# The scan of a two-layer sequence kernel: z, v and u moved by pairs of octets

## The chip, the cores and the metric

The kernel runs on one core of one Trainium2 chip. The metric is the device time of one execution in microseconds, as a median over runs. Before the change it is 2332.63 us, median of 3 runs that lie between 2332.56 and 2332.96.

The core has TensorE (PE, with its weight loads shown apart as PEld), VectorE (DVE), ScalarE (ACT), GpSimd (POOL) and SyncE (SP). SP does no arithmetic here; it issues nearly all DMA transfers, in program order.

## The reference

Two layers over x (2 batches, 4096 positions, 512 channels, f32). The change lies in the first layer, in its recurrence:

```python
Abar = sigmoid(A)                      # A: 512 channels x 16 states
def step(h, xt):                       # h: batch x channels x states
    h = h * Abar + xt[..., None] * B_ssm
    y = einsum('bcs,cs->bc', h, C_ssm) + D_ssm * xt
    return (h, y)
x1 = x @ w1_w.T + w1_b
x_ssm = _ssm(silu(_depthwise_conv(x1, conv_w)), A, B_ssm, C_ssm, D_ssm)
v = silu(x @ v1_w.T + v1_b)
return x_ssm * v @ w2_w.T + w2_b
```

Beside it the first layer has a product with weights and inputs quantised to a 6-bit grid in blocks of 32; the second has a linear attention with 16 heads and a gated feed-forward net. Both layers start with a layer norm and add onto x.

## The kernel before, in words

The program has four phases one after the other, with a barrier of all engines between them: project (`x @ w1`, `x @ v1`, convolution, silu; results go to DRAM as `scr_z` and `scr_v`), scan (the recurrence), mix (the rest of layer 1 and the start of layer 2) and second_layer. The change is in scan, `phase_scan` at L509, which takes from 418.04 to 608.76 us of the profiled span.

The scan works on octets: 8 channels at a time, so 64 octets (`NO`). The 4096 positions of a batch are cut into chunks of 16. For one octet, z is a tile of 128 partitions (8 channels x 16 places in a chunk) by 512 columns (2 batches x 256 chunks), 256 KB in f32. The work on octet o is:

- POOL spreads three tables of the octet into 128x128 matrices: `into`, `toep`, `outof` (L580, three tables in turn, `TABS`).
- PE `own(o)` (L673): z times `into`, into one of two banks `SB`. It gives each chunk's own contribution to the state at its end.
- DVE `scan(o)` (L590): two scans along the chunks give the `state`.
- PE `Y(o)`, as this text calls it: z times `toep` (L690) and then `state` times `outof` (L693), both into one of two banks `YB`.
- DVE `gate(o)` (L596): `YB` times v, written over v. This is u.

A product of f32 appears in the trace as two matmul records. PE runs in the order own(o+1), Y(o); DVE in the order scan(o+1), gate(o). In the first nine octets DVE also does one step of the quantisation of a weight after each gate (L610 to L632; five of the nine take about 2.3 us); ACT loads four weight matrices of 1 MB at the start of the phase (L654 to L658), and PE turns one of them in octets 24 to 27 (L680).

SP loads z (`zo`, 4 buffers) and v (`vo`, 5 buffers), one transfer of 256 KB per octet each, and stores u from the v buffer. `load(o)` waits, for a z buffer, until the Y that read it is complete (`y_full`), and for a v buffer until the store of u from it has landed (`u_stored`). Octets 0 to 3 are loaded at once; after that, each turn of SP's loop waits for gate(o) (`u_done`), stores u of o, and loads octet o+4 (`load(o + 3)` at the head of the next turn). The phase ends when all stores have landed (L568).

Of the kernel before, what the change touches and what calls it, by code (L numbers as in the profile page):

```python
# [3 lines left out]
P = 128  # L4
# [3 lines left out]
ALU = mybir.AluOpType  # L8
# [16 lines left out]
OCTET = 8  # L25
# [483 lines left out]
def phase_scan(nc, sh, ins, scr, keep, banks, mem, late):  # L509
    KT, D, NO, NCB, NCH, NS, B = sh.KT, sh.D, sh.NO, sh.NCB, sh.NCH, sh.NS, sh.B  # L510
    sb = mem.tile
    Z, V, TABS = 4, 5, 3

    def sem(name):
        return nc.alloc_semaphore(name)

    zo = [sb(f"c_z{i}", [P, NCH]) for i in range(Z)]
    vo = [sb(f"c_v{i}", [P, NCH]) for i in range(V)]
    state = [sb(f"c_state{i}", [P, B, NCB]) for i in range(2)]
    into = [sb(f"c_into{i}", [P, OCTET, NS]) for i in range(TABS)]  # L520
    toep = [sb(f"c_toep{i}", [P, OCTET, CHUNK]) for i in range(TABS)]
# [9 lines left out]
    z_in = [sem(f"c_z_in{i}") for i in range(Z)]  # L531
    v_in = [sem(f"c_v_in{i}") for i in range(V)]
    u_stored = [sem(f"c_u_stored{i}") for i in range(V)]
# [3 lines left out]
    y_full, u_done = sem("c_y_full"), sem("c_u_done")  # L537
# [5 lines left out]
    SB, YB, FB = banks[0:2], banks[2:4], banks[4:8]  # L543
    into_t, toep_t, out_pow, mask8 = keep["into_t"], keep["toep_t"], keep["out_pow"], keep["mask8"]
    ident = keep["ident"]
    z_of = scr["z"].rearrange("(o c) r n -> o (c r) n", c=OCTET)
    v_of = scr["v"].rearrange("(o c) m n -> o (c m) n", c=OCTET)
    u_of = scr["u"].rearrange("(o c) m n -> o (c m) n", c=OCTET)
    TURN_AT = 24

    def sync(sp):
        def load(o):
            if o >= Z:
                sp.wait_ge(y_full, o - Z + 1)
            sp.dma_start(zo[o % Z][:, :], z_of[o]).then_inc(z_in[o % Z], 16)
            if o >= V:
                sp.wait_ge(u_stored[o % V], 16 * (o // V))
            sp.dma_start(vo[o % V][:, :], v_of[o]).then_inc(v_in[o % V], 16)

        for o in range(3):  # L560
            load(o)
        for o in range(NO):
            if o + 3 < NO:
                load(o + 3)
            sp.wait_ge(u_done, o + 1)
            sp.dma_start(u_of[o], vo[o % V][:, :]).then_inc(u_stored[o % V], 16)
        for i in range(V):
            sp.wait_ge(u_stored[i], 16 * len(range(i, NO, V)))  # L568

    def gpsimd(pool):  # L570
        nc.gpsimd.memset(keep["kv"][:, :, :, :], 0.0).then_inc(keep["set"], 1)
# [11 lines left out]
    def vector(dve):  # L583
        def scan(o):
            dve.wait_ge(own_full, o + 1)
            if o >= 2:
                dve.wait_ge(y_full, o - 1)
            rate = keep["decay"][:, o:o + 1].broadcast_to([P, NCB - 1])
            for b in range(B):
                nc.vector.tensor_tensor_scan(state[o % 2][:, b, 1:], rate, SB[o % 2][:, b * NCB:(b + 1) * NCB - 1],  # L590
                                             0.0, ALU.mult, ALU.add).then_inc(state_done, 1)

        def gate(o):
            dve.wait_ge(y_full, o + 1)
            dve.wait_ge(v_in[o % V], 16 * (o // V + 1))
            nc.vector.tensor_tensor(vo[o % V][:, :], YB[o % 2][:, :], vo[o % V][:, :], ALU.mult).then_inc(u_done, 1)  # L596

        def weight_low(i, kt, tile, raw):
            dve.wait_ge(w_hi, KT * i + kt + 1)
            nc.vector.tensor_tensor(tile[:, 1, kt, :], raw[:, kt, :], tile[:, 0, kt, :].bitcast(F32),  # L600
                                    ALU.subtract).then_inc(w_lo, 1)

        blocks = wf_nat[:, :].rearrange("p (b e) -> p b e", e=QBLOCK)
        NB = KT * D // QBLOCK

        def wide(tile):
            return tile[:, :].unsqueeze(2).broadcast_to([P, NB, QBLOCK])

        def quantise_step(k):
            dve.wait_ge(wf_in, 16)  # L610
            if k:
                dve.wait_ge(q_step, k)
            if k == 0:
                ins_ = nc.vector.tensor_reduce(q_max[:, :], blocks, AX.X, ALU.max, apply_absolute_value=True)
            elif k == 1:
                ins_ = nc.vector.tensor_scalar(q_scale[:, :], q_max[:, :], 1.0 / FP6_MAX, SCALE_EPS, ALU.mult, ALU.max)
            elif k == 2:
                ins_ = nc.vector.reciprocal(q_inv[:, :], q_scale[:, :])
            elif k == 3:
                ins_ = nc.vector.tensor_tensor(blocks, blocks, wide(q_inv), ALU.mult)  # L620
            elif k == 4:
                ins_ = nc.vector.tensor_scalar(q_work[:, :].bitcast(U32), wf_nat[:, :].bitcast(U32), EXPONENT_BITS,
                                               None, ALU.bitwise_and)
            elif k == 5:
                ins_ = nc.vector.tensor_scalar(q_work[:, :], q_work[:, :], 1.0, ROUND_MAGIC, ALU.max, ALU.mult)
            elif k == 6:
                ins_ = nc.vector.tensor_tensor(wf_nat[:, :], wf_nat[:, :], q_work[:, :], ALU.add)
            elif k == 7:
                ins_ = nc.vector.tensor_tensor(wf_nat[:, :], wf_nat[:, :], q_work[:, :], ALU.subtract)
            else:  # L630
                ins_ = nc.vector.tensor_tensor(blocks, blocks, wide(q_scale), ALU.mult)
            ins_.then_inc(q_step, 1)  # L632

        for i in range(2):
            nc.vector.memset(state[i][:, :, 0:1], 0.0).then_inc(zeroed, 1)
        dve.wait_ge(zeroed, 2)
        scan(0)
        for o in range(NO):
            if o + 1 < NO:
                scan(o + 1)  # L640
            gate(o)
            if o < 9:
                quantise_step(o)
            if TURN_AT <= o - 2 < TURN_AT + KT:
                kt = o - 2 - TURN_AT
                dve.wait_ge(f_hi, kt + 1)
                nc.vector.tensor_tensor(wf[:, 1, kt, :], FB[kt][:, :], wf[:, 0, kt, :].bitcast(F32), ALU.subtract)\
                  .then_inc(w_lo, 1)
            if 32 <= o < 32 + 2 * KT:
                i, kt = divmod(o - 32, KT)  # L650
                weight_low(i, kt, *((w2, w2_raw), (wk, wk_raw))[i])
# [14 lines left out]

    def tensor(pe):
        def own(o):
            pe.wait_ge(z_in[o % Z], 16 * (o // Z + 1))
            pe.wait_ge(tab_done, 3 * (o + 1))  # L670
            if o >= 2:
                pe.wait_ge(state_done, B * (o - 1))
            pe.matmul(SB[o % 2][:, :], into[o % TABS][:, :, :].rearrange("p c s -> p (c s)"), zo[o % Z][:, :],  # L673
                      start=True, stop=True).then_inc(own_full, 1)

        def turn_weight(kt):
            if kt == 0:
                pe.wait_ge(q_step, 9)
            for ot in range(KT):
                mm = pe.transpose(FB[kt][:, ot * P:(ot + 1) * P], wf_nat[:, ot * D + kt * P:ot * D + (kt + 1) * P],  # L680
                                  ident[:, :])
            mm.then_inc(f_turned, 1)

        own(0)
        for o in range(NO):
            if o + 1 < NO:
                own(o + 1)
            if o >= 2:
                pe.wait_ge(u_done, o - 1)
            pe.matmul(YB[o % 2][:, :], toep[o % TABS][:, :, :].rearrange("p c m -> p (c m)"), zo[o % Z][:, :],  # L690
                      start=True, stop=False)
            pe.wait_ge(state_done, B * (o + 1))
            pe.matmul(YB[o % 2][:, :], outof[o % TABS][:, :, :].rearrange("p c m -> p (c m)"),  # L693
                      state[o % 2][:, :, :].rearrange("p b n -> p (b n)"), start=False, stop=True).then_inc(y_full, 1)
            if TURN_AT <= o < TURN_AT + KT:
                turn_weight(o - TURN_AT)

    return sync, gpsimd, vector, scalar, tensor


# [911 lines left out]
def two_layer_kernel(nc, ins, out):  # L1612
# [60 lines left out]
    for name in ("w2", "wf", "wk"):  # L1673
# [3 lines left out]

    run_phase(nc, "project", phase_project(nc, sh, ins, scr, keep, banks, Stretch(nc, after_tables)))
    run_phase(nc, "scan", phase_scan(nc, sh, ins, scr, keep, banks,
                                     Stretch(nc, after_tables, SBUF_END - 9 * weight), late))  # L1680
    run_phase(nc, "mix", phase_mix(nc, sh, ins, scr, keep, banks,
# [46 lines left out]
```

## Time and profile before

| what | value |
|---|---|
| time, median of 3 runs | 2332.63 us |
| the profiled execution's own time | 2332.52 us |
| span of its instructions | 2330.9 us |
| mean granted TensorE clock | 0.978 |
| busy: PE, DVE, ACT, POOL | 2148.1 us (92%), 1595.5 (68%), 1023.5 (44%), 852.4 (37%) |
| DMA in all | 241.40 MB, mean 104 GB/s |
| scan phase | 418.04 to 608.76 us |

How to read it: the profile is one execution, and its span runs from the first to the last instruction; the execution's own time is 1.6 us longer. "Busy" is the time in which an engine has an instruction in work. Granted clock is the share of the full TensorE clock, so 1.00 is 2.4 GHz and 0.50 is 1.2 GHz. A transfer's time "to landing" is from its issue to the last of its data.

### The profile page before, as it was taken

How to read it: one execution, taken by the hardware profiler on the slowest of the kernel's cores; microseconds unless marked ns; L12 is line 12 of the kernel's file. 1: busy time of each engine (PE TensorE's matmuls, PEld its weight loads, DVE VectorE, ACT ScalarE, POOL GpSimd, SP SyncE). 2: the span in 40 equal slices, each digit the busy share in tenths (PEclk: the TensorE clock that was granted, in tenths of full speed). 3: DMA queues.
4: the chain of work that ended last, by engine and by line, in shares of the span. 5: the costliest groups of instructions: out<-in, count | busy, mean ns of one | idle time of the engine just before them, and what ended most of it. 6: DMA issues, size and time to landing. Idle time of an engine off the chain costs nothing. (4 is left out here: it accounts for less than half of the span.)

```text
span 2330.9 us, 27638 instructions
## 1 busy us (share of the span) xinstructions
PE 2148.1 (92%) x9466; PEld 1665.1 (71%) x9466; DVE 1595.5 (68%) x2983; ACT 1023.5 (44%) x1705; POOL 852.4 (37%) x838
## 2 busy tenths in 40 slices
PE   7999998699699999999999999599999999999997
PEld 5888887244377777777877777477777887778886
DVE  5576554778677777777677776267776777766775
ACT  3445545100145454555544544264454444555442
POOL 0030000344344444444444444024343444343443
PEclk9999999799899999999999999799999999999999
DMA  3244432789422222222232221221222112222111
GB/s 139 101 142 134 142 129 104 269 294 303 167 91 73 88 76 85 79 73 89 91 101 82 73 90 51 90 86 64 96 77 82 64 64 66 97 87 68 64 37 37
DMA packets 165462, 241.40 MB, mean 104 GB/s; under 512 B 19273, under 2 KB 93257, under 8 KB 164170
## 3 DMA queue, kind: packets, MB, share of 16 engines
q1 hardware_dynamic: 162760, 231.31, 29.7%
q10 hardware_dynamic: 2562, 8.32, 1.0%
q8 instruction: 76, 1.25, 0.2%
q14 instruction: 64, 0.52, 0.1%
HBM read 138.86 MB, written 100.73 MB: 103 GB/s over the span
## 5 line engine op out<-in xcount | busy, mean ns | idle before, releaser
L95 PE MATMUL bank<-e_ring,e_w_hi 128*128 128x512 f32 x512 | 207.0, 404 | 17.7 <-DVE e_ring L1425 16.7
L96 PE MATMUL bank<-e_ring,e_w_hi 128*128 128x512 f32 x512 | 205.5, 401 | 0.0
L1110 PE MATMUL bank<-d_kh,d_nat 128*128 128x512 f32 x768 | 197.4, 407 | 8.5 <-DVE d_kh L1009 7.6
L97 PE MATMUL bank<-e_ring,e_w_lo 128*128 128x512 f32 x512 | 200.5, 392 | 0.0
L1425 DVE TENSOR_TENSOR e_ring<-e_mixed,e_ring 128x512 fp32r<-128x512 f32 x128 | 95.9, 749 | 151.4 <-ACT e_ring L1323 151.4
L1306 POOL TENSOR_TENSOR e_x<-e_x,e_ff 128x512 f32<-128x512 f32 x64 | 82.5, 1289 | 238.3 <-DVE e_ff L1474 238.3
L1110 PEld LDWEIGHTS bank<-d_kh,d_nat 128*128 128x128 f32 x768 | 142.0, 192 | 38.3 <-issue 9.7
L973 DVE TENSOR_TENSOR d_qt<-bank,d_qt 128x512 fp32r<-128x512 f32 x64 | 44.3, 692 | 177.7 <-ACT d_qt L875 177.7
L1354 ACT ACTIVATE e_kr<-bank 128x512 f32<-128x512 f32 x64 | 38.0, 594 | 290.7 <-PE bank L97 235.8
L1300 POOL TENSOR_TENSOR e_x<-e_x,e_beta 128x512 f32<-128x512 f32 x64 | 83.5, 1305 | 224.1 <-ACT e_y L1345 224.1
L842 POOL TENSOR_TENSOR d_kacc<-d_kacc,d_kr 128x512 f32<-128x512 f32 x64 | 82.6, 1291 | 223.4 <-ACT d_kr L902 223.4
L824 POOL TENSOR_TENSOR d_xq<-d_xq,d_magic 128x512 f32<-128x512 f32 x64 | 83.1, 1299 | 219.0 <-DVE d_xq L1005 219.0
L95 PE MATMUL bank<-d_wf,d_qt 128*128 128x512 f32 x256 | 107.8, 421 | 49.7 <-DVE d_qt L973 47.1
L221 POOL TENSOR_TENSOR b_rstd<-b_var_eps,neg_half 128x4 f32<-128x4 f32 x16 | 16.1, 1009 | 324.2 <-DVE b_var_eps L262 324.2
L95 PEld LDWEIGHTS bank<-e_ring,e_w_hi 128*128 128x128 f32 x512 | 96.4, 188 | 51.2 <-DVE e_ring L1425 18.9
L95 PE MATMUL bank<-e_w_hi,e_ring 128*128 128x512 f32 x256 | 102.1, 399 | 22.0 <-DVE e_ring L1425 22.0
L924 ACT ACTIVATE d_xn<-d_x,shift,rstd 128x512 f32<-128x512 f32 x64 | 52.3, 817 | 159.4 <-POOL shift L865 159.4
L1418 DVE SCALAR_TENSOR_TENSOR e_mixed<-e_xt,cols,e_prev 128x512 f32<-128x512 f32 x128 | 103.2, 806 | 20.9 <-ACT e_prev L1332 20.3
L1009 DVE TENSOR_TENSOR d_kh<-d_kr,d_kh 128x512 fp32r<-128x512 f32 x64 | 87.7, 1371 | 43.1 <-ACT d_kh L905 43.1
L97 PEld LDWEIGHTS bank<-e_ring,e_w_lo 128*128 128x128 f32 x512 | 97.0, 189 | 23.0
L273 DVE TENSOR_TENSOR b_xt<-bank,b_xt 128x512 fp32r<-128x512 f32 x64 | 43.9, 688 | 98.7 <-ACT b_xt L378 98.5
L96 PEld LDWEIGHTS bank<-e_ring,e_w_hi 128*128 128x128 f32 x512 | 96.9, 189 | 19.7
(208 smaller groups left out, 6442.5 us busy)
## 6 DMA issues: line engine op xcount, KB each, us to landing
b_xg<-in_L_attn_x SPq DMA_DIRECT2D x32, 512.0 KB, 4.8
scr_v<-b_vt SPq DMA_DIRECT2D x64, 256.0 KB, 2.7
scr_z<-b_zt SPq DMA_DIRECT2D x64, 256.0 KB, 2.1
c_z<-scr_z SPq DMA_DIRECT2D x64, 256.0 KB, 2.9
c_v<-scr_v SPq DMA_DIRECT2D x64, 256.0 KB, 3.1
scr_u<-c_v SPq DMA_DIRECT2D x64, 256.0 KB, 2.3
d_x<-in_L_attn_x SPq DMA_DIRECT2D x64, 256.0 KB, 3.0
d_ut_raw<-scr_u SPq DMA_DIRECT2D x32, 512.0 KB, 3.7
```

What stands on the lines that cost most here:

```text
L95: eng.matmul(out, lhs[hi], rhs[hi], start=first, stop=False, skip_group_check=onto)
L96: eng.matmul(out, lhs[hi], rhs[lo], start=False, stop=False, skip_group_check=onto)
L97: return eng.matmul(out, lhs[lo], rhs[hi], start=False, stop=last, skip_group_check=onto)
L824: nc.gpsimd.tensor_tensor(tile[:, :], tile[:, :], magic[:, N % 2, :], ALU.subtract).then_inc(q_sub, 1)
L842: nc.gpsimd.tensor_tensor(kacc[b][:, :], kacc[b][:, :], kr[M % 2][:, :], ALU.add).then_inc(kacc_done, 1)
L924: nc.scalar.activation(xn[N % 2][:, :], x2[N % Q][:, :], ACT.Identity, scale=keep["rstd1"][:, N:N + 1], bias=keep["shift1"][:, N:N + 1]).t ...
L1009: nc.vector.tensor_tensor(kh[M % 2][:, 1, :], kr[M % 2][:, :], kh[M % 2][:, 0, :].bitcast(F32), ALU.subtract).then_inc(k_lo, 1)
L1110: mm = pe.matmul(BG[c][:, :], s[:, i, cols], r[:, j, :], start=M % NTB == 0 and i == j, stop=M % NTB == NTB - 1 and i == 1, skip_group_che ...
L1300: nc.gpsimd.tensor_tensor(x2[h][:, t, :], x2[h][:, t, :], beta[:, :], ALU.add).then_inc(shifted, 1)
L1306: nc.gpsimd.tensor_tensor(x2[h][:, t, :], x2[h][:, t, :], ff[t % 2][:, :], ALU.add)\
L1418: nc.vector.scalar_tensor_tensor(mixed[kt % 2][:, :], current(g % 2, kt), mu[:, kt:kt + 1], prev[kt % 2][:, :], ALU.mult, ALU.add).then_in ...
L1425: nc.vector.tensor_tensor(ring[slot][:, 1, kt, :], src, ring[slot][:, 0, kt, :].bitcast(F32), ALU.subtract).then_inc(lo_done, 1)
```

## The change

z and v are loaded, and u is stored, for two octets in one transfer: 512 KB, with two rows of 2 KB per partition. There are 96 transfers where there were 192; the bytes are the same. Each of z and v has three buffers of a pair (6 octets each) where there were 4 and 5 buffers of one. The arithmetic, its order on PE, DVE, ACT and POOL, and the tables are as before; PE and DVE take their half of a pair's tile.

```diff
-    Z, V, TABS = 4, 5, 3
+    Z, V, TABS = 3, 3, 3
-    zo = [sb(f"c_z{i}", [P, NCH]) for i in range(Z)]
-    vo = [sb(f"c_v{i}", [P, NCH]) for i in range(V)]
+    zp = [sb(f"c_z{i}", [P, 2, NCH]) for i in range(Z)]
+    vp = [sb(f"c_v{i}", [P, 2, NCH]) for i in range(V)]
-    z_of = scr["z"].rearrange("(o c) r n -> o (c r) n", c=OCTET)
+    z_of = scr["z"].rearrange("(o h c) r n -> o (c r) h n", h=2, c=OCTET)
...
     def sync(sp):
-        def load(o):
-            if o >= Z:
-                sp.wait_ge(y_full, o - Z + 1)
-            sp.dma_start(zo[o % Z][:, :], z_of[o]).then_inc(z_in[o % Z], 16)
-            if o >= V:
-                sp.wait_ge(u_stored[o % V], 16 * (o // V))
-            sp.dma_start(vo[o % V][:, :], v_of[o]).then_inc(v_in[o % V], 16)
-
-        for o in range(3):
-            load(o)
-        for o in range(NO):
-            if o + 3 < NO:
-                load(o + 3)
-            sp.wait_ge(u_done, o + 1)
-            sp.dma_start(u_of[o], vo[o % V][:, :]).then_inc(u_stored[o % V], 16)
+        def load(pair):
+            if pair >= Z:
+                sp.wait_ge(y_full, 2 * (pair - Z) + 2)
+            sp.dma_start(zp[pair % Z][:, :, :], z_of[pair]).then_inc(z_in[pair % Z], 16)
+            if pair >= V:
+                sp.wait_ge(u_stored[pair % V], 16 * (pair // V))
+            sp.dma_start(vp[pair % V][:, :, :], v_of[pair]).then_inc(v_in[pair % V], 16)
+
+        for pair in range(2):
+            load(pair)
+        for pair in range(NO // 2):
+            if pair + 2 < NO // 2:
+                load(pair + 2)
+            sp.wait_ge(u_done, 2 * pair + 2)
+            sp.dma_start(u_of[pair], vp[pair % V][:, :, :]).then_inc(u_stored[pair % V], 16)
...
         def gate(o):
             dve.wait_ge(y_full, o + 1)
-            dve.wait_ge(v_in[o % V], 16 * (o // V + 1))
-            nc.vector.tensor_tensor(vo[o % V][:, :], YB[o % 2][:, :], vo[o % V][:, :], ALU.mult).then_inc(u_done, 1)
+            pair, mine = o // 2, vp[o // 2 % V][:, o % 2, :]
+            dve.wait_ge(v_in[pair % V], 16 * (pair // V + 1))
+            nc.vector.tensor_tensor(mine, YB[o % 2][:, :], mine, ALU.mult).then_inc(u_done, 1)
...
         def own(o):
-            pe.wait_ge(z_in[o % Z], 16 * (o // Z + 1))
+            pe.wait_ge(z_in[o // 2 % Z], 16 * (o // 2 // Z + 1))
```

The order of SP at the start of the scan, before. `c_z` and `c_v` are the z and v buffers, `scr_u` is u in DRAM; a wait stands with the instruction behind it.

```order
68 L555 DMA c_z_4012<-scr_z 128x512
69 L558 DMA c_v_4016<-scr_v 128x512
70 L555 DMA c_z_4013<-scr_z 128x512
71 L558 DMA c_v_4017<-scr_v 128x512
72 L555 DMA c_z_4014<-scr_z 128x512
73 L558 DMA c_v_4018<-scr_v 128x512
74 L555 DMA c_z_4015<-scr_z 128x512
75 L558 DMA c_v_4019<-scr_v 128x512
76 L566 DMA scr_u<-c_v_4016 128x512 [waits c_u_done]
77 L555 DMA c_z_4012<-scr_z 128x512 [waits c_y_full]
78 L558 DMA c_v_4020<-scr_v 128x512
```

And the same place after the change:

```order
68 L555 DMA c_z_4012<-scr_z 128x2x512
69 L558 DMA c_v_4015<-scr_v 128x2x512
70 L555 DMA c_z_4013<-scr_z 128x2x512
71 L558 DMA c_v_4016<-scr_v 128x2x512
72 L555 DMA c_z_4014<-scr_z 128x2x512
73 L558 DMA c_v_4017<-scr_v 128x2x512
74 L566 DMA scr_u<-c_v_4015 128x2x512 [waits c_u_done]
75 L555 DMA c_z_4012<-scr_z 128x2x512 [waits c_y_full]
76 L558 DMA c_v_4015<-scr_v 128x2x512 [waits c_u_stored0]
77 L566 DMA scr_u<-c_v_4016 128x2x512 [waits c_u_done]
```

Six octets stand ahead of the first wait where four did, and the load of v in row 76 now waits for the store in row 74, two rows ahead of it in the same queue. Before, SP in its loop reused the v buffer of the store before the last:

```order
79 L566 DMA scr_u<-c_v_4017 128x512 [waits c_u_done]
80 L555 DMA c_z_4013<-scr_z 128x512 [waits c_y_full]
81 L558 DMA c_v_4016<-scr_v 128x512 [waits c_u_stored0]
```

There the buffer 4016 was stored in row 76, and the store in row 79 went to another one.

On PE the instructions keep their order; what changes is the transfer that a product waits for. The start of the scan before:

```order
1667 L673 MATMUL bank<-c_z_4012,c_into_4023 128x512 [waits c_tab_done,c_z_in0]
1668 L673 MATMUL bank<-c_z_4013,c_into_4024 128x512 [waits c_tab_done,c_z_in1]
1669 L690 MATMUL bank<-c_z_4012,c_toep_4026 128x512
1670 L693 MATMUL bank<-c_state_4021,c_outof_4029 128x512 [waits c_state_done]
1671 L673 MATMUL bank<-c_z_4014,c_into_4025 128x512 [waits c_state_done,c_tab_done,c_z_in2]
```

And after the change:

```order
1667 L674 MATMUL bank<-c_z_4012,c_into_4020 128x512 [waits c_tab_done,c_z_in0]
1668 L674 MATMUL bank<-c_z_4012,c_into_4021 128x512 [waits c_tab_done,c_z_in0]
1669 L691 MATMUL bank<-c_z_4012,c_toep_4023 128x512
1670 L694 MATMUL bank<-c_state_4018,c_outof_4026 128x512 [waits c_state_done]
1671 L674 MATMUL bank<-c_z_4013,c_into_4022 128x512 [waits c_state_done,c_tab_done,c_z_in1]
```

own(0) and own(1) now wait for the first transfer, and own(2) for the second z transfer of SP's queue, which is its third transfer in all.

## Rows read from the trace of the kernel before

**Rows 1.** Windows: busy us (instructions) of each engine, PEclk, DMA share, GB/s.
```profile
418.00:434.00 16.00, 7.17 (x8) 2.35 (x8) 2.61 (x6) 4.38 (x8) 4.22 (x10) 0.50 0.93 363
434.00:435.00 1.00, 1.00 (x3) 0.55 (x3) 0.57 (x1) 0.00 (x0) 0.53 (x2) 0.77 1.04 402
443.00:465.00 22.00, 18.19 (x41) 7.25 (x40) 22.00 (x26) 0.00 (x0) 12.87 (x20) 1.00 0.74 240
478.00:504.00 26.00, 26.00 (x65) 11.71 (x64) 19.56 (x31) 0.48 (x1) 11.48 (x32) 1.00 0.92 305
```
**Rows 2.** Waits, 418 to 609 us: total, times, longest; DMA for PE, then SP's own.
```profile
PE bank L673 <- DMA c_z<-scr_z: 28.4, 6, 19.6
...
SPq L566 <- DVE c_v L596: 102.2, 64, 12.8
...
SPq L558 <- DMA scr_u<-c_v: 1.4, 3, 0.6
```
**Rows 3.** Timeline of the start: start us, us, engine, line, what [idle before].
```profile
421.86 0.45 SPq L558 DMA_DIRECT2D c_v<-scr_v  x1
...
428.91 2.07 PE L673 MATMUL bank<-c_z,c_into 128*128 128x512 f32 x2 [6.11 <-DMA c_z<-scr_z]
430.77 1.92 PE L690 MATMUL bank<-c_z,c_toep 128*128 128x512 f32 x2
...
434.21 1.23 PE L673 MATMUL bank<-c_z,c_into 128*128 128x512 f32 x2
...
441.29 1.02 PE L693 MATMUL bank<-c_state,c_outof 128*128 128x512 f32 x2
...
442.40 0.67 DVE L596 TENSOR_TENSOR c_v<-bank,c_v 128x512 f32<-128x512 f32 x1
```
**Rows 4.** Line L558: longest time to landing of the c_v loads.
```profile
DMA to landing us min/median/max: 2.9/3.1/14.2
```
**Rows 5.** Timeline of PE after the quantisation.
```profile
465.25 1.02 PE L673 MATMUL bank<-c_z,c_into 128*128 128x512 f32 x2
466.11 1.02 PE L690 MATMUL bank<-c_z,c_toep 128*128 128x512 f32 x2
...
468.23 1.12 PE L673 MATMUL bank<-c_z,c_into 128*128 128x512 f32 x2 [0.23 <-DMA c_z<-scr_z]
...
471.88 1.12 PE L673 MATMUL bank<-c_z,c_into 128*128 128x512 f32 x2 [0.81 <-DMA c_z<-scr_z]
```
**Rows 6.** Timeline of SP in the steady part: stores of u.
```profile
480.63 0.32 SPq L566 DMA_DIRECT2D scr_u<-c_v  x1
...
503.81 0.32 SPq L566 DMA_DIRECT2D scr_u<-c_v  x1
504.17 0.43 SPq L555 DMA_DIRECT2D c_z<-scr_z  x1
...
569.94 0.32 SPq L566 DMA_DIRECT2D scr_u<-c_v  x1
...
583.93 0.32 SPq L566 DMA_DIRECT2D scr_u<-c_v  x1
```
**Rows 7.** DMA issues: queue, count, KB each, median us to landing.
```profile
c_z<-scr_z SPq DMA_DIRECT2D x64, 256.0 KB, 2.9
...
scr_u<-c_v SPq DMA_DIRECT2D x64, 256.0 KB, 2.3
...
scr_xnt<-d_xt SPq DMA_DIRECT2D x32, 512.0 KB, 4.1
...
out<-e_x SPq DMA_DIRECT2D x32, 512.0 KB, 3.3
```
**Rows 8.** The end of the scan and the start of mix: timeline, then a window.
```profile
605.52 0.69 DVE L596 TENSOR_TENSOR c_v<-bank,c_v 128x512 f32<-128x512 f32 x1 [1.02 <-PE bank L693]
608.76 0.33 SPq L785 DMA_DIRECT2D d_x<-in_L_attn_x  x1
...
608.50:630.00 21.50, 5.55 (x16) 4.15 (x17) 13.06 (x20) 5.82 (x8) 9.73 (x9) 0.52 0.43 135
```

More of the change, by code:

```diff
@@ L545, in phase_scan @@
     ident = keep["ident"]
-    z_of = scr["z"].rearrange("(o c) r n -> o (c r) n", c=OCTET)
-    v_of = scr["v"].rearrange("(o c) m n -> o (c m) n", c=OCTET)
-    u_of = scr["u"].rearrange("(o c) m n -> o (c m) n", c=OCTET)
+    z_of = scr["z"].rearrange("(o h c) r n -> o (c r) h n", h=2, c=OCTET)
+    v_of = scr["v"].rearrange("(o h c) m n -> o (c m) h n", h=2, c=OCTET)
+    u_of = scr["u"].rearrange("(o h c) m n -> o (c m) h n", h=2, c=OCTET)
     TURN_AT = 24
     def sync(sp):
-        def load(o):
-            if o >= Z:
-                sp.wait_ge(y_full, o - Z + 1)
-            sp.dma_start(zo[o % Z][:, :], z_of[o]).then_inc(z_in[o % Z], 16)
-            if o >= V:
-                sp.wait_ge(u_stored[o % V], 16 * (o // V))
-            sp.dma_start(vo[o % V][:, :], v_of[o]).then_inc(v_in[o % V], 16)
-        for o in range(3):
-            load(o)
-        for o in range(NO):
-            if o + 3 < NO:
-                load(o + 3)
-            sp.wait_ge(u_done, o + 1)
-            sp.dma_start(u_of[o], vo[o % V][:, :]).then_inc(u_stored[o % V], 16)
+        def load(pair):
[12 more added lines that the diff above has]
+            sp.dma_start(u_of[pair], vp[pair % V][:, :, :]).then_inc(u_stored[pair % V], 16)
         for i in range(V):
-            sp.wait_ge(u_stored[i], 16 * len(range(i, NO, V)))
+            sp.wait_ge(u_stored[i], 16 * len(range(i, NO // 2, V)))
     def gpsimd(pool):
@@ L672, in own @@
                 pe.wait_ge(state_done, B * (o - 1))
-            pe.matmul(SB[o % 2][:, :], into[o % TABS][:, :, :].rearrange("p c s -> p (c s)"), zo[o % Z][:, :],
+            pe.matmul(SB[o % 2][:, :], into[o % TABS][:, :, :].rearrange("p c s -> p (c s)"), zp[o // 2 % Z][:, o % 2, :],
                       start=True, stop=True).then_inc(own_full, 1)
@@ L689, in tensor @@
                 pe.wait_ge(u_done, o - 1)
-            pe.matmul(YB[o % 2][:, :], toep[o % TABS][:, :, :].rearrange("p c m -> p (c m)"), zo[o % Z][:, :],
+            pe.matmul(YB[o % 2][:, :], toep[o % TABS][:, :, :].rearrange("p c m -> p (c m)"), zp[o // 2 % Z][:, o % 2, :],
                       start=True, stop=False)
```

## The prediction

> **What bounds the kernel now.** I read the windows first, then the waits, then the timeline of the scan from its start, and last the DMA issues. The change touches 190.7 us of the span, so the first question is what sets the pace of an octet there. The windows [rows 1] show three regimes.
>
> At the start, 418 to 434 us, PE is busy for 7.17 of 16 us at half clock while the DMA engines run at 0.93 of their time and 363 GB/s: the phase waits for data, since ACT's four weight matrices (4 MB) come in beside SP's loads. From 443 to 465 DVE is busy for all 22.00 us: the quantisation steps bound the octets. From 478 on PE is busy all the time at full clock. The stores of u, one per octet, show the steady pace: from 480.63 to 503.81 there are nine octets in 23.18 us, 2.576 each [rows 6]. That is three products of 0.86, the distance from 465.25 to 466.11 [rows 5]. DMA is at 0.92 of its time there with 305 GB/s, near its limit but not the bound: 402 GB/s are reached from 434 to 435 [rows 1].
>
> PE's waits for z [rows 2] sum to 28.4 us, but one of them is the 19.6 us ahead of the first octet, and 6.1 more stand ahead of the second [rows 3]. What is left inside the loop is small. SP waits 102.2 us for gates and only 1.4 us for stores: the issuing queue has plenty of free time, so fewer issues by themselves gain nothing.
>
> **The change part by part.** The sums are made against the profiled execution, 2332.52 us, which stands 0.1 below the median of the runs.
>
> *Issues.* 96 fewer, of 0.32 to 0.45 us each [rows 6], some 37 us of SP's time. All of it lies in SP's wait for gates. Worth 0.
>
> *First data.* own(2) waits for z of octet 2. Before, this was the fifth transfer, 1.25 MB into SP's queue, and own(2) began at 434.21 [rows 3]. Now it needs the third transfer of 512 KB, 1.5 MB into the queue, one 256 KB piece more. The last of the first eight transfers, 2 MB in, was issued at 421.86 and took 14.2 us, the longest of its line [rows 3, 4]: it landed at 436.0. So three pieces took 436.0 - 434.2 = 1.8 us, 0.6 each, which also is 256 KB at 402 GB/s [rows 1]. own(2) moves to 434.8: +0.6. The first octet itself gains nothing: own(1), the first gate and the first quantisation step can all come earlier, but the next thing for PE is own(2), and its data come when the weights are through.
>
> *The clock.* PE ran at the half level (0.50, 1.2 GHz) from 418 to 434 and rose within 434 to 435, where the mean is 0.77 [rows 1]. It had been busy without a gap since 428.91, about 5.5 us [rows 3]. Now own(0), own(1) and Y(0) are four products of 1.9 and 3 x 1.7 us at half clock (428.91 to 430.77, and two in the 3.4 to 434.21), 7 us in all, and follow right on the first transfer. That transfer is the first two pieces of 256 KB. Before, the third piece was there at 428.9 and the fifth at 434.2, 2.65 us each, which puts the second at 426.3 or earlier. The products end by 433.3, earlier if it lands earlier, and then PE stands still until 434.8. That no full clock outlives such a pause is suggested by the next phase, where PE does little and the clock is 0.52 [rows 8]. So own(2) should start at half clock. No row shows how soon it rises: the bounds are 0 (it is up all the same) and 5.5 us (as long as before), and I take 3 us, about the middle. Half clock for 3 us loses 1.5 us of PE's work, for 5.5 us 2.75. Does DVE hide it? Y(3)'s last product began at 441.29 and ran 1.02, to 442.31; gate(3) began at 442.40 [rows 3]. PE and DVE arrive there together, with 0.1 us of slack, and behind it DVE is the bound with no idle time [rows 1]. So the delay goes through but for 0.1: +1.4, bounds 0 and +2.7.
>
> The Trainium skill, in "TensorE: Matmul & The Clock Gate", section "HAM oscillation — how this bites in real kernels", tells the same mechanism: a pause for DMA between two bursts of products puts TensorE back to its half clock, and the next burst starts slow. The row of the next phase agrees, but has no burst behind its pause. With the rule the sum is the one below; if the rule doesn't bite here, the term is 0 (rival A).
>
> *z behind the quantisation.* When DVE lets go, PE runs ahead of the loads: own(13) began at 468.23 and own(14) at 471.88, both behind a wait for z [rows 5]. From own(12) at 465.25 two octets at PE's pace end at 465.25 + 2 x 2.58 = 470.4, so 1.5 us were lost. With pairs these z are asked for earlier. Before, the load of z(k) was issued behind gate(k-4), and between the end of Y(k-4) and own(k) stand six products, 5.15 us. Of these 1.1 go to the gate (0.69, [rows 8]) and to the store's issue ahead of the load (0.37 from 503.81 to 504.17, [rows 6]); 4.1 are left for a landing of 2.9 [rows 7]. Now the pair 2p is asked for behind gate(2p-5), nine products ahead: 7.7 - 1.1 = 6.6 us. Its landing: no z of 512 KB is in the trace; from 256 to 512 KB a store goes from 2.3 to 3.3, so +1.0 on 2.9, and the 512 KB of u ahead of it in place of 256 KB, +0.6, makes 4.5 (an estimate). 2.1 us are spare instead of 1.2. The wait goes: -1.5, bounds -1.5 and 0.
>
> *Late disturbances.* Between 569.94 and 583.93 five octets took 13.99 us in place of 12.88 [rows 6]: z was late by 1.1. The wider reserve takes it: -1.1, bounds -1.1 and 0.
>
> *The added wait.* SP now waits with the load of v for the store that it issued two transfers earlier. Behind this wait stand the next store and the next load of z. A pair lasts 5.15 us. The store takes 3.3 us (the nearest row, `out`, 512 KB stored) or 4.1 (`scr_xnt`) [rows 7]; then 0.45 for the issue of v. 3.3 + 0.5 = 3.8, or 4.6, is below 5.15, so SP is back in time for the next gate. v itself is issued some 4 us behind the gate of octet 2p-5 and lands by 8.5 us, and gate(2p) comes 12.9 us behind that. Worth 0.
>
> *The end.* The last store now carries 512 KB and starts behind the last gate as before (605.52, next phase at 608.76) [rows 8]. By the medians it lands 3.3 - 2.3 = 1.0 later, by `scr_xnt` 1.8, at the least 0.5: +1.0.
>
> Sum: 0.6 + 1.4 - 1.5 - 1.1 + 1.0 = +0.4 us. 2332.52 + 0.4 is 2332.9, against the median 2333.0.
>
> **The rivals.**
>
> *A: the clock doesn't matter.* It is up at own(2), and all other terms stand: 0.6 - 1.5 - 1.1 + 1.0 = -1.0, 2331.6. For it: the first burst of four products at half clock may lift the clock late. Against it: no row shows a full clock over a pause of this kind.
>
> *B: SP's new wait becomes the bound.* It decides when a store of 512 KB takes more than 5.15 - 0.5 = 4.65 us in the middle of the loop, with a load of 512 KB queued behind it and DMA at 0.9 of its time. The longest store of 256 KB took 4.4 us (the median is 2.3). If the median went to 5.0, each pair would last 5.5, +0.35 over the 26 pairs of the steady part: +9 us, with the start's terms about 2342. For it: DMA at 0.92. Against it: at 402 GB/s 1.5 MB take 3.9 of 5.15 us, so the queue empties once in each pair.
>
> *C: larger transfers speed the whole scan up.* The Trainium skill, in "DMA: Bandwidth & Descriptors", section "Rules for kernel authors", asks for large transfers, 1 MiB and up, for bandwidth. As a mechanism of this kernel: fewer and larger transfers bring data faster, and what waits for DMA shrinks. The start cannot (the weights come at 363 GB/s and more already), and in the loop only PE's waits can go, 1.5 + 1.1 and some tenths: at best about -3.5 with nothing on the other side, 2329.0. Faster than that would need PE to beat 2.58 per octet.
>
> *D: the start is worse.* The first pair of z, 512 KB, shares the queue with the weights, and the clock stays at half for 5.5 us: 0.6 + 2.7, no gain later (z in pairs comes late too), the end +1.8: +5.1, 2337.7.
>
> **How the numbers follow.** The forecast has a chance of 0.45, A 0.28, B 0.07, C 0.08, D 0.12. A change of 0.2% is 4.7 us, about what a measurement of this kernel can tell from none. The forecast, A, and C lie within it, D at its edge (half of it beyond). Faster by more is a part of C, if it also shortens the start: 0.05. Slower: B and half of D, 0.12. Same: 0.83. The range takes A and reaches towards C on one side and takes D's nearer part on the other: 2330.0 to 2337.5. Outside it lie most of C, B, and a third of D, with what no row shows together about 0.2.
>
> **What would show it.** The load of v behind its store: SP's wait for stores goes from 1.4 to roughly 32 x 2.5 = 80 us, and its wait for gates shrinks, with stores of u 5.15 us apart in the steady part. own(2) begins near 434.8 behind a wait for z, and the clock in the window 434 to 438 is near 0.5 (A: near 1.0). No wait of PE for z behind 440. The last gate starts at 605.52 + 0.6 + 1.4 - 1.5 - 1.1 = 604.9, and the next phase at 609.2. The forecast is wrong if PE is idle in the steady part, if pairs last over 5.2 us, or if a phase behind the scan changes its length.

## The result, and the profile after

The changed kernel takes 2345.13 us, median of 5 runs (2342.56 to 2345.42); the kernel before, 2332.56 us (2329.44 to 2332.96). The ratio is 1.0054, with a 95% interval from 1.0043 to 1.0066: slower by 12.6 us. Forecast were 2333.0 us, with a range from 2330.0 to 2337.5. Of the rivals B came true, at more than its price (about 2342).

Nearly all of it is in the scan. Mix starts at 622.38 us of the span where it started at 608.76 [rows 8], 13.6 later; the scan itself starts at 418.41 in place of 418.04, 0.4 later, so it takes 204.0 us in place of 190.7, 13.2 more. Behind the scan the profile of the changed kernel is 1.3 us shorter, but over the profiles of this case that stretch, with the same work in it, varies from 1719.6 to 1722.3 us. First, the windows of the kernel after, in the form of [rows 1].

```profile
418.00:434.00 16.00, 6.71 (x9) 2.79 (x10) 5.49 (x8) 3.38 (x7) 5.34 (x13) 0.61 0.91 353
...
435.00:438.00 3.00, 3.00 (x4) 1.01 (x3) 1.26 (x2) 0.00 (x0) 0.00 (x0) 0.50 1.04 405
...
443.00:465.00 22.00, 19.19 (x43) 7.54 (x41) 21.69 (x25) 0.00 (x0) 12.94 (x19) 1.00 0.79 253
490.00:565.00 75.00, 71.19 (x172) 30.42 (x172) 57.79 (x90) 2.39 (x4) 32.78 (x78) 1.00 0.84 273
```

The stretch of the quantisation is as it was. In the steady part (478 to 504 us before, 490 to 565 now), where PE had no idle time and DMA moved 305 GB/s at 0.92, PE now is idle for 3.8 of 75 us by its modelled ends, and DMA moves 273 GB/s at 0.84. Neither is at its limit. The waits from 417 to 625 us, first PE's for z, then SP's own (total, times, longest), name what holds them up:

```profile
PE bank L674 <- DMA c_z<-scr_z: 33.7, 21, 22.0
...
SPq L558 <- DMA scr_u<-c_v: 115.8, 29, 5.6
SPq L566 <- DVE c_v L597: 38.8, 7, 18.2
```

In [rows 2] SP waited 102.2 us for gates and 1.4 for stores. Now it waits 115.8 us for stores, at each of the 29 loads of v behind the first three, and found the gate done for all but 7 stores. SP's timeline shows one turn of the loop after the other:

```profile
500.83 0.36 SPq L558 DMA_DIRECT2D c_v<-scr_v  x1
501.24 0.47 SPq L566 DMA_DIRECT2D scr_u<-c_v  x1
501.75 0.47 SPq L555 DMA_DIRECT2D c_z<-scr_z  x1
506.55 0.36 SPq L558 DMA_DIRECT2D c_v<-scr_v  x1
506.95 0.47 SPq L566 DMA_DIRECT2D scr_u<-c_v  x1
507.47 0.47 SPq L555 DMA_DIRECT2D c_z<-scr_z  x1
512.30 0.36 SPq L558 DMA_DIRECT2D c_v<-scr_v  x1
512.70 0.47 SPq L566 DMA_DIRECT2D scr_u<-c_v  x1
```

From store to store (501.24, 506.95, 512.70) a pair takes 5.7 us, not 5.15. The three issues of a turn stand within a microsecond, v, u, z; then SP waits until this u has landed, 5.3 us after its issue. The DMA issues (KB each, median us to landing) agree:

```profile
c_z<-scr_z SPq DMA_DIRECT2D x32, 512.0 KB, 6.0
...
scr_u<-c_v SPq DMA_DIRECT2D x32, 512.0 KB, 5.3
```

And the windows of two turns show why DMA is below its limit. The three transfers of a turn run together at 378 to 389 GB/s; when they end, near 507, SP has only just issued the next three (506.55 to 507.94), nothing else is queued, and for about two us little moves.

```profile
503.50:506.50 3.00, 3.00 (x8) 1.33 (x7) 2.38 (x5) 0.00 (x0) 1.13 (x3) 1.00 1.03 383
507.00:509.00 2.00, 2.00 (x9) 1.14 (x8) 0.86 (x3) 0.60 (x1) 1.12 (x3) 1.00 0.40 103
509.00:512.50 3.50, 3.50 (x12) 1.72 (x11) 2.44 (x4) 0.60 (x1) 1.13 (x3) 1.00 1.01 378
513.00:515.00 2.00, 2.00 (x9) 1.15 (x8) 1.53 (x4) 0.60 (x1) 1.12 (x3) 1.00 0.63 129
515.00:518.00 3.00, 3.00 (x11) 1.53 (x10) 2.54 (x4) 0.60 (x1) 1.13 (x3) 1.00 1.01 389
```

The stores of u place the loss. Octet 1 was stored at 439.09 before and its pair at 439.85 now, +0.8; octet 3 at 443.10 and 445.00, +1.9; octet 9 at 464.85 and 466.63, +1.8; octet 13 at 475.48 and 477.87, +2.4; the last at 606.24 and 619.26, +13.0. Of the 1.9 us of the start 0.4 lie ahead of the scan, so the start costs 1.5; nearly all the rest comes from the steady part, behind octet 13.

### The profile page after: what moved, and what is told of

Read it like the earlier page. It is cut to its first block and busy times, and to the rows that moved or that the text cites. A ratio compares the mean times of both kernels' runs of the same rounds, so it can differ in the third digit from the quotient of the medians.

```text
span 2343.2 us, 27541 instructions
## 1 busy us (share of the span) xinstructions
PE 2153.3 (92%) x9466; PEld 1665.7 (71%) x9466; DVE 1596.1 (68%) x2983; ACT 1023.2 (44%) x1705; POOL 852.6 (36%) x838
## 3 DMA queue, kind: packets, MB, share of 16 engines
q8 instruction: 76, 1.25, 0.2%
```

## The experiments

Theory 1: SP's wait for the store that it has just issued closes a loop, and the loop is the bound. Theory 2: transfers of 512 KB with two rows a quarter MB apart are slower by themselves. "The median of before" is that of the runs beside the experiment.

**Four v buffers.** The wait is then for the store of the turn before the last.

```diff
-    Z, V, TABS = 3, 3, 3
+    Z, V, TABS = 3, 4, 3
```

> The changed kernel with four pair buffers for v in place of three, so that the load of v waits for the store of the turn before the last, not for the one just issued. Theory 1, the wait for the just issued store closes a loop (store lands, v issued, next store issued, 5.3 us to landing): the steady pairs go from 5.78 to 5.15 us, SP's wait for stores from 115.8 to under 10 us, DMA share in the steady part up, time 2331 to 2334. Theory 2, transfers of 512 KB with two rows a quarter MB apart move data more slowly: the pairs stay near 5.7 us, c_z and scr_u still land in over 5 us, time 2343 to 2346.

Measured: 2331.33 us against 2331.88 before, ratio 0.9999 (0.9991 to 1.0008). Its windows, waits and issues:

```profile
516.00:570.00 54.00, 54.00 (x127) 23.90 (x126) 46.46 (x74) 0.00 (x0) 27.07 (x64) 1.00 0.89 305
```
```profile
SPq L566 <- DVE c_v L597: 133.4, 32, 18.2
...
PE bank L674 <- DMA c_z<-scr_z: 25.9, 2, 22.1
```
```profile
c_z<-scr_z SPq DMA_DIRECT2D x32, 512.0 KB, 4.7
...
scr_u<-c_v SPq DMA_DIRECT2D x32, 512.0 KB, 3.3
```

SP waits for gates alone, PE waits for z only ahead of own(0) and own(2), and the same 512 KB store lands in 3.3 us. Theory 2 is out. One buffer of 512 KB is worth about 13 us: 12.6 above the kernel before without it, 0.5 below with it, each against the runs beside it.

**Three v buffers, v issued behind the next store.**

```diff
...
+            if pair and pair + 2 < NO // 2:
+                load_z(pair + 2)
             sp.wait_ge(u_done, 2 * pair + 2)
             sp.dma_start(u_of[pair], vp[pair % V][:, :, :]).then_inc(u_stored[pair % V], 16)
+            if pair and pair + 2 < NO // 2:
+                load_v(pair + 2)
```

> The changed kernel, still with three pair buffers for v, but in each turn of SP the load of v (with its wait for a store) is issued behind the next store instead of ahead of it. Theory 1 (the loop store, wait, v, next store): the wait finds a store that is 5 us old, the pairs take 5.15 us, 2331 to 2335. Theory 2 (the transfers are slow by themselves): 2343 to 2346. A third, three buffers are too few however SP orders them (v then comes late for its gate): PE or DVE waits for c_v appear, and the time stays over 2338.

Measured: 2336.34 us, ratio 1.0021 (1.0012 to 1.0029). The wait for stores is gone and u lands in 3.3 us again, but 4.5 us of the loss stay, over the upper end of what was expected. The third theory's waits for c_v do not appear. What the trace does show is z, which now stands behind both u and v:

```profile
530.72 0.36 SPq L569 DMA_DIRECT2D scr_u<-c_v  x1
531.13 0.47 SPq L560 DMA_DIRECT2D c_v<-scr_v  x1
531.64 0.75 SPq L555 DMA_DIRECT2D c_z<-scr_z  x1
```
```profile
PE bank L679 <- DMA c_z<-scr_z: 28.3, 6, 22.1
```
```profile
c_z<-scr_z SPq DMA_DIRECT2D x32, 512.0 KB, 5.5
```

z lands in 5.5 us in place of 4.7, and is issued 0.9 us behind u in place of 0.4 with four buffers: PE waits for it in the loop four times, 2.2 us in all by its modelled ends. That accounts for half of the 4.5; the profile is of the shortest of the eleven executions, 2334.71, and where the rest goes is open. That z ahead of v would win this back with three buffers is likely from these rows, but no run shows it.

**Octets, four v buffers.** The kernel before, with the same kind of wait.

```diff
-    Z, V, TABS = 4, 5, 3
+    Z, V, TABS = 4, 4, 3
```

> The kernel before, transfers of one octet, but with four v buffers in place of five, so that here too the load of v waits for the store issued just ahead of it. Theory 1: the loop is there without pairs; a store of 256 KB with a load ahead of it lands in about 3 us, plus 0.45 of issue gives at least 3.3 us per octet in place of 2.58, over some 50 octets +35 us, about 2368. Theory 2 (only the 512 KB form is slow): no change beyond 5 us, about 2333.

Measured: 2378.21 us, ratio 1.0200 (1.0186 to 1.0214), +46. SP's waits and a piece of its timeline:

```profile
SPq L558 <- DMA scr_u<-c_v: 132.2, 60, 2.8
```
```profile
529.83 0.43 SPq L566 DMA_DIRECT2D scr_u<-c_v  x1
530.31 0.43 SPq L555 DMA_DIRECT2D c_z<-scr_z  x1
532.75 0.32 SPq L558 DMA_DIRECT2D c_v<-scr_v  x1
533.11 0.43 SPq L566 DMA_DIRECT2D scr_u<-c_v  x1
```

The loop is the same with 256 KB: 3.3 us from store to store in this piece in place of 2.58, and a wait for a store at each of the 60 loads of v behind the first four. The loop is not a matter of pairs. From octet 13 to octet 60 an octet takes 3.56 us on average, where it took 2.64 before (480.59 to 647.91, and 475.48 to 599.38); that is 1.8 per two octets. With pairs, from octet 13 to octet 59, a pair takes 5.77 with three buffers (477.87 to 610.53) and 5.23 with four (476.07 to 596.27), so the loop costs 0.5. A turn of 512 KB takes less than two turns of 256 KB, 5.77 against 7.1: part of the round trip does not grow with the bytes.

**z in pairs alone**, v and u per octet with five buffers.

```diff
-    Z, V, TABS = 4, 5, 3
+    Z, V, TABS = 3, 5, 3
...
-            sp.dma_start(zo[o % Z][:, :], z_of[o]).then_inc(z_in[o % Z], 16)
+            sp.dma_start(zp[pair % Z][:, :, :], z_of[pair]).then_inc(z_in[pair % Z], 16)
```

> One part of the change alone: z in pairs (three pair buffers), v and u per octet with five buffers as before. Theory 1: no wait for a just issued store, so the steady pace is PE's, 2330 to 2334, and z late behind the quantisation and at the late disturbances goes. Theory 2: z in 512 KB transfers lands late by itself, PE waits for z in the steady part, 2337 or more.

Measured: 2331.59 us, ratio 0.9998 (0.9989 to 1.0007), and no wait of PE for z behind own(2). This part of the change is harmless; with the run of four v buffers, it is v's three buffers that cost.

**Does the loop need a push?** In the changed kernel it closed when the pair behind the quantisation came 4.2 us after the one before (470.88 after 466.63). Here the quantisation steps work on 64 of 2048 columns, with three v buffers; the rest of that weight stays unquantised.

```diff
-        blocks = wf_nat[:, :].rearrange("p (b e) -> p b e", e=QBLOCK)
-        NB = KT * D // QBLOCK
+        NB = 2
+        blocks = wf_nat[:, 0:NB * QBLOCK].rearrange("p (b e) -> p b e", e=QBLOCK)
...
```

> The changed kernel with three v buffers, with the quantisation steps cut to 64 of 2048 columns (the rest of that weight is left unquantised). DVE is then never the bound, and there is no quick pair behind the quantisation (in the changed kernel the store of octets 10 and 11 follows 3.9 us behind the one before, and from there on every v load goes out directly ahead of a store). Theory 1a, the loop has two states and needs such a push: stores stay 5.15 us apart, scru_u lands in 3.3 us, the next phase starts at about 600. Theory 1b, the loop closes by itself: stores 5.7 to 5.8 us apart from early on, and the next phase starts at about 615.

Measured, one run: 2339.69 us; mix starts at 617.61. SP's timeline, stores and loads of v:

```profile
440.74 0.36 SPq L566 DMA_DIRECT2D scr_u<-c_v  x1
...
443.75 0.36 SPq L558 DMA_DIRECT2D c_v<-scr_v  x1
446.18 0.36 SPq L566 DMA_DIRECT2D scr_u<-c_v  x1
...
449.75 0.36 SPq L558 DMA_DIRECT2D c_v<-scr_v  x1
...
461.62 0.36 SPq L566 DMA_DIRECT2D scr_u<-c_v  x1
...
466.08 0.36 SPq L558 DMA_DIRECT2D c_v<-scr_v  x1
466.77 0.36 SPq L566 DMA_DIRECT2D scr_u<-c_v  x1
...
472.14 0.36 SPq L558 DMA_DIRECT2D c_v<-scr_v  x1
472.55 0.47 SPq L566 DMA_DIRECT2D scr_u<-c_v  x1
```

Four pairs run at 5.15 us, from the store at 446.18 to the one at 466.77. But the way from a store to the load of v behind it grows turn by turn: 3.0 us, 3.6, 3.9, 4.1, 4.5, 5.4. The later v is issued, the closer it stands ahead of the next store, and the later that lands. At 472.14 v goes out directly ahead of the store, and from there on a pair takes 5.8 us. No quick pair was needed, so theory 1a falls as it was stated. 1b holds for the end state, 5.8 us per pair, though the loop closes over several turns and not from early on. One push is left in both kernels: in the turn of the last step SP's issue of z took 1.61 us in place of 0.47, and the one at 467.04 in the changed kernel took 1.74; the traces do not say why. Whether the way would have stayed at 4.5 without it is open, and so is whether the loop closes with no disturbance at all.

**PE kept busy over the start's pause** (four v buffers, four products that nobody reads).

```diff
+            if o == 0:
+                for _ in range(4):
+                    pe.matmul(FB[3][:, :], ident[:, :], zp[0][:, 0, :], start=True, stop=True)
```

> The kernel with pairs and four v buffers, plus four products (identity times z of octet 0, into a bank that is not used yet) behind Y(0), to fill PE's pause before own(2). If the half clock at own(2) costs what the changed kernel's start lost (the clock fell in the pause and stayed at half for some 5 us): the window from 434 to 438 shows a clock near 1.0, the second store of u moves from 445.4 to about 443, and the time falls by 2 us. If the clock falls all the same or DVE bounds the start: no change.

Measured: 2328.92 us against 2332.17, ratio 0.9986 (0.9977 to 0.9996). The window of the start:

```profile
434.00:438.00 4.00, 4.00 (x10) 1.71 (x9) 3.12 (x6) 0.65 (x2) 1.12 (x3) 1.00 1.01 394
```

The clock is 1.00 where the changed kernel had 0.50, and the second store of u comes at 442.01, where the version without the products had it at 445.39: 3.4 us. Of these 0.5 are an earlier start of the scan (418.04 in place of 418.54) and 0.2 an earlier z (own(2) at 433.26 in place of 433.94, 0.7 in all). The half clock at own(2) is shown to cost 2.7 us here. Mix starts at 605.52, after a scan of 187.5 us where the version without took 190.3.

**The late weights.** Three of ACT's four loads wait for the 3rd, 5th and 7th octet; with pairs and four v buffers, and in the kernel before.

```diff
+        act.wait_ge(y_full, 3)
         act.dma_start(w2_raw[:, :, :], ins["L0_attn_w2_w"]).then_inc(raw_in[0], 16)
+        act.wait_ge(y_full, 5)
         act.dma_start(wk_raw[:, :, :], ins["L1_attn_Wk"]).then_inc(raw_in[1], 16)
+        act.wait_ge(y_full, 7)
         act.dma_start(wv[:, :, :], ins["L1_attn_Wv"]).then_inc(late["wv_in"], 16)
```

> The kernel with pairs and four v buffers; of ACT's four loads of 1 MB at the start of the scan, three wait for the 3rd, 5th and 7th octet. Theory: the start waits for bytes, so with 3 MB less ahead own(2) starts near 426 in place of 433.6, and the time falls by 6 to 8 us to about 2324. If those weights then hold up z during the quantisation, PE waits for z appear between 440 and 460 and less is gained.

> The kernel before (one octet per transfer, five v buffers) with the same three weights loaded late. It tells what part of the gain needs pairs: by the theory that pairs are neutral without the wait, also about 2324; z has less reserve here, so up to 3 us more.

Measured: 2327.95 us with pairs, ratio 0.9979 (0.9970 to 0.9988), and 2330.94 with octets, 0.9996 (0.9987 to 1.0006). Both expectations were missed. With pairs 4.2 us are gained of 6 to 8. own(2) started at 430.17 and not near 426: it had no wait for z left, but own(0) came no sooner, at 423.91 (423.65 with four buffers alone), and PE's products at half clock filled the time between. Then comes what the expectation's second case had:

```profile
443.97 2.08 PE L677 MATMUL bank<-c_z,c_into 128*128 128x512 f32 x2 [3.21 <-DMA c_z<-scr_z]
```

PE waited for z beside the weights and went on at half clock, 2.08 us for a product in two records. How much of this the other executions had is not shown: the profile is of the longest of the ten executions, 2331.65, and its scan took 190.4 us, no less than without late weights. With octets nothing clear of noise is gained, where 2324 to 2327 was expected; own(2) starts at 430.82, and behind it PE waits for z seven times, the longest 2.3 us. So with late weights pairs come out 3.0 us ahead of octets, at intervals that just touch.

**The weights in quarters, and the end.** Twelve loads of 256 KB behind octets 3 to 14, four buffers each for z and v; in the second version also the last pair's u stored by octets.

```diff
+        at = 3
...
+            for kt in range(KT):
+                act.wait_ge(y_full, at)
+                act.dma_start(tile[:, kt, :], ins[name][:, kt, :]).then_inc(done, 16)
+                at += 1
```

> Pairs with four buffers each for z and v, and the three late weights in twelve loads of 256 KB, one behind each of the octets 3 to 14. In the version with late loads of 1 MB, PE waited 3.2 us for z at 444 and its clock fell, since the weights ran beside it. If it was the size and the speed at which they were asked for, PE doesn't wait for z here between 430 and 465, the second store of u comes near 439 and the next phase starts near 604; 2325 to 2328. If any weight traffic in that stretch holds up z, the wait stays and the time is 2328 or more.

> The same, and u of the last pair is stored octet by octet. By the forecast's term for the end (512 KB land 1.0 us later than 256 KB) it gains 1.0 us on the version without; if the end of the phase doesn't hang on the size of the last store, nothing.

Measured: 2327.98 us against 2333.64, ratio 0.9977 (0.9968 to 0.9986), and 2328.70, 0.9981 (0.9973 to 0.9990). The first beats both kernels, by 5.7 us the one before, but it does not beat the late loads of 1 MB. Its time is at the upper end of what was expected, and PE still waited for z between 430 and 465, once for 1.46 us at 442.42, at full clock; mix starts at 606.74, not near 604. The second version was expected to gain 1.0 us and did not: the intervals do not tell the two apart. Their traces do for the end alone. The last store and the first issue of mix, in the first and then in the second:

```profile
594.15 9.80 SPq L566 DMA_DIRECT2D scr_u<-c_v  x3
606.74 0.35 SPq L790 DMA_DIRECT2D d_x<-in_L_attn_x  x1
```
```profile
604.69 0.33 SPq L569 DMA_DIRECT2D scr_u<-c_v  x1
607.15 0.34 SPq L797 DMA_DIRECT2D d_x<-in_L_attn_x  x1
```

The last of the three stores was issued at 594.15 + 9.80 - 0.36 = 603.59, so 3.15 us pass to mix, and 2.46 with 256 KB: 0.7 us less.

## Why the prediction was wrong

**The step that failed is "The added wait".** It took the store's landing from rows of other phases (3.3 and 4.1 us), where the DMA engines are busy for 0.27 of the time (610 to 1200 us of the kernel before) and 0.21 (from 1200), and found 3.8 or 4.6 below 5.15, "Worth 0". The price of a store with no load directly ahead of it was right: 3.3 us, with four buffers and with v issued late. But the wait itself sets what travels beside it. v is issued when the store has landed, and the next store stands behind v in the same queue; so a store lands not 3.3 but 5.3 us after its issue, and 5.3 + 0.45 = 5.75 is the pair's length that was measured (5.77 on average from the store at 477.87 to that at 610.53, 23 pairs). It is the load ahead that counts: in the run with v issued late both v and z stand directly behind u, and u lands in 3.3. Of the 2.0 us that v ahead adds, its 512 KB explain 1.4 at 378 GB/s (an estimate from the windows); the rest is not split up by any run. The check "below 5.15" had to be made for this arrangement, v directly ahead of u. Rival B named the mechanism and a fair threshold, 4.65 us, but gave it 0.07 by the same rows, and argued against it that the queue empties once in each pair. It does, and that is the loss and not a reserve: nothing more is issued until the store has landed, so the two us between a turn's issues and its data (507 to 509, 103 GB/s) are paid in every pair.

**First data, +0.6.** own(2) began at 433.61, and the whole phase 0.37 later than before, so z of the second pair was there 1.0 us earlier than z of octet 2 had been, not 0.6 later. The pace within the queue while weights run beside it was misread: the term is -1.0, with the wrong sign in the forecast. Why 1.5 MB were there sooner than 1.25 MB had been is open.

**The clock, +1.4.** The mechanism is right and shown by the experiment with four extra products. The clock had just risen, the product at 428.70 took 1.04 us; PE stood idle from 429.7 to 433.61, the clock was 0.50 until 438, and the timeline of PE after shows it:

```profile
428.70 1.04 PE L694 MATMUL bank<-c_state,c_outof 128*128 128x512 f32 x2
433.61 2.07 PE L674 MATMUL bank<-c_z,c_into 128*128 128x512 f32 x2 [3.87 <-DMA c_z<-scr_z]
435.48 1.91 PE L691 MATMUL bank<-c_z,c_toep 128*128 128x512 f32 x2
437.18 1.92 PE L694 MATMUL bank<-c_state,c_outof 128*128 128x512 f32 x2
438.89 1.07 PE L674 MATMUL bank<-c_z,c_into 128*128 128x512 f32 x2
```

The half level lasted 5.3 us (433.61 to 438.89), near the upper bound and not the 3 us taken: 2.65 of PE's work. The pause was misjudged too: the forecast had 1.5 us or more (433.3 to 434.8), and it was 3.9, since PE had the first pair at 423.42. What follows a pause of 1.5 us no version shows at this place; in the version with quarters PE waited 1.46 us at 442.42 and the clock stayed up, the product behind it took 1.12. The two errors nearly cancel, by luck: first data and clock together were forecast as +2.0, and from the start of the scan octet 3 is stored 1.5 late.

**z behind the quantisation, -1.5, and late disturbances, -1.1.** Both are there as soon as the loop is open. With four v buffers PE has no wait for z in the loop, z lands in 4.7 us (4.5 estimated), and from the store of octet 3 to the last one the scan takes 160.3 us where it took 163.1: -2.8. With +1.8 from the start and +0.6 from the end that makes -0.4, and the scan takes 190.3 us in place of 190.7. In the changed kernel the gain was eaten by the closed loop. The second term was read a little high: of its 1.1 us the kernel before shows 0.66 as PE's wait for z, at 580.33.

**The end, +1.0.** From the last store to mix it is 3.1 us in place of 2.5 before, and the pair of runs with and without the small last store has 3.15 and 2.46: 0.6 to 0.7.

**Issues, 0.** Right as far as shown: SP's queue had free time, and the version with 96 issues fewer and four buffers gains nothing clear of noise (0.9999). No run tests the issues alone.

Without the added wait the forecast's sum, +0.4, stands against -0.5 measured with four buffers, with an interval of about 2 us to either side. That it is so near is partly luck, by the two errors at the start. The chance written down for slower, 0.12, is 0.13 by its own terms (0.07 and half of 0.12), which changes nothing.

## What to carry to other kernels

When a queue waits for a transfer that it has issued itself, price the wait by the round trip with everything that the wait then places ahead of the next such transfer, not by the transfer's time alone, and ask whether the queue stands empty meanwhile. The distance between a store and the reuse of its buffer is counted in transfers: going from five small buffers to three large ones took it from two stores to one here, though it holds more data. One more buffer was worth about 13 us; the pairs themselves, nothing as the kernel stood, and about 3 us once the weights were loaded late.

## What the runs showed of the hardware

A loop of this kind can look open at first: store to v load grew from 3.0 to 4.5 us over five turns at an unchanged pace, and only then did the pace fall. Where the load stands counts: a store of 512 KB landed in 3.3 us (median) with two loads of 512 KB directly behind it, and in 5.3 with one 0.4 us ahead of it and one behind. A pause of 3.9 us of PE between products was followed by 5.3 us at the half level, 1.2 GHz, with PE busy throughout; four products in that pause kept it at 2.4 GHz.
